# Half of the causal masks moved from a matmul to GpSimd, as a product on the exponentials' bits

## The reference

```
q = LN(x) @ Wq.T + bq ; k = ctx @ Wk.T + bk ; v = ctx @ Wv.T + bv
scores = einsum("bgrqd,bgkd->bgrqk", q, k) / sqrt(8)
scores = where(causal_mask, -inf, scores)      # 128 x 128, the same for all
scores = where(padding_mask, -inf, scores)     # 8 x 128, one row per batch
w   = softmax(scores)
x   = x + tanh(g_xattn) * ((w @ v) @ Wo.T + bo)
x   = x + tanh(g_ffn) * moe(LN(x))             # router, top 2 of 16, silu(gate) * up, down
```

## Time and profile before

| | us |
|---|---|
| median of three runs | 269.31 |
| span of the profiled execution (first to last instruction) | 267.6 |
| PE busy, share of the span | 237.8, 89% |
| DVE busy | 188.0, 70% |
| ACT busy | 96.7, 36% |
| POOL busy | 90.8, 34% |
| mean granted TensorE clock | 0.959 |

### The profile page before, as it was taken

How to read it: one execution, slowest core, us unless ns; L and a number is a source line. 1 busy time by engine, 2 the same in 40 slices (tenths; PEclk the granted TensorE clock), 3 DMA queues, 4 the chain that set the end, 5 groups by cost and what they waited for, 6 DMA issues and landing times.

```text
span 267.6 us, 3780 instructions
## 1 busy us (share of the span) xinstructions
PE 237.8 (89%) x1275; PEld 168.9 (63%) x1275; DVE 188.0 (70%) x388; ACT 96.7 (36%) x173; POOL 90.8 (34%) x103
## 2 busy tenths in 40 slices
PE   0874889897789999999968999989999999999993
PEld 0751345454546555556544588768888888888883
DVE  2689786958877777675793377769767665766565
ACT  1575023857746565564546521111111010101000
POOL 6266008030081417361160110406936633562000
PEclk9997556999999999999999999999999999999998
DMA  7945400001100000211011000001322102000004
GB/s 208 159 129 127 109 1 2 0 0 43 39 0 1 2 0 7 55 21 37 1 26 35 1 2 0 0 0 39 82 61 60 38 21 61 0 0 2 0 0 158
DMA packets 20595, 10.25 MB, mean 38 GB/s; under 512 B 14400, under 2 KB 20064, under 8 KB 20576
## 3 DMA queue, kind: packets, MB, share of 16 engines
q1 hardware_dynamic: 20272, 9.79, 15.5%
q10 hardware_dynamic: 304, 0.22, 0.3%
HBM read 7.91 MB, written 1.05 MB: 33 GB/s over the span
## 4 chain that ended last, share of the span: by engine, by line
PE 74%; DVE 14%; ACT 5%; issue 3%; DMA 2%; ACTq 0%; DVEq 0%
PE bank L878 66%; ACT q L527 3%; PE bank L939 2%; DMA wkv_n<-in_L_xattn_Wv 2%; DVE q L629 2%; PE bank L918 2%; DVE mneg L740 2%; PE bank L935 1%; DVE xn L620 1%; DVE x_sb L871 1%; DVE w L782 1%; PE bank L952 1%; DVE xT L626 1%; PE bank L944 1%; DVE k L629 1%
## 5 line engine op out<-in xcount | busy, mean ns | idle before, releaser
L878 PE MATMUL bank<-xT,cT 128*128 128x512 f32 x288 | 70.2, 392 | 0.0
L878 PEld LDWEIGHTS bank<-xT,cT 128*128 128x128 f32 x288 | 53.7, 188 | 12.0 <-issue 0.8
L740 DVE TENSOR_REDUCE mneg<-bank 128x4 f32<-128x512 f32 x64 | 43.7, 687 | 19.6 <-PE bank L878 18.9
L585 ACT ACTIVATE pT<-bank 128x512 f32<-128x512 f32 x64 | 38.3, 601 | 28.4 <-PE bank L878 27.3
L572 ACT ACTIVATE pT<-bank 128x512 f32<-128x512 f32 x24 | 14.4, 598 | 84.2 <-PE bank L878 84.2
L878 PEld LDWEIGHTS bank<-w_d,q 128*128 128x128 f32 x288 | 37.1, 188 | 2.8 <-issue 1.3
L878 PE MATMUL bank<-q,kz 112*128 112x512 f32 x64 | 38.8, 609 | 0.0
L878 PE MATMUL bank<-w_d,q 128*128 128x256 f32 x288 | 38.0, 281 | 0.8 <-DVE q L818 0.8
L878 PE MATMUL bank<-kz,q 96*128 96x512 f32 x64 | 30.6, 484 | 5.9 <-DVE mneg L740 3.2
L411 POOL TENSOR_TENSOR vare<-mv,cst 128x1 f32<-128x1 f32 (+1 forms) x10 | 1.9, 194 | 82.4 <-DVE mv L614 80.4
L878 PE MATMUL bank<-cmask,ident_b 128*128 128x512 bf16 x64 | 28.4, 444 | 0.0
(11 more groups left out here) (119 smaller groups left out, 312.0 us busy)
## 6 DMA issues: line engine op xcount, KB each, us to landing
padf<-in_L_ffn_down_w SPq DMA_DIRECT2D x12, 128.0 KB, 2.3
c_sb<-in_ctx SPq DMA_DIRECT2D x2, 512.0 KB, 7.3
q<-q SPq DMA_DIRECT2D x8, 128.0 KB, 2.4
out<-x_sb SPq DMA_DIRECT2D x4, 256.0 KB, 2.4
c_sb<-in_L_ffn_gate_w SPq DMA_DIRECT2D x8, 96.0 KB, 2.2
c_sb<-in_L_ffn_up_w SPq DMA_DIRECT2D x8, 96.0 KB, 2.2
x_sb<-in_x SPq DMA_DIRECT2D x2, 256.0 KB, 3.6
x_sb<-in_x SPq DMA_DIRECT2D x1, 512.0 KB, 8.0
```

The costliest lines, as they stand in the source:

```text
L585: nc.scalar.activation(pT[:, i // 4, i % 4, :], bank[2 + s % 2][:], ACT.Exp, scale=SCALE).then_inc(p_done, 1)
L740: nc.vector.tensor_reduce(mneg[:, r, 4 * hf:4 * hf + 4], bank[n % 2][:].rearrange("p (g k) -> p g k", g=4), X, ALU.max, negate=True).then_ ...
L878: return nc.tensor.matmul(dst, a, b, start=start, stop=stop, skip_group_check=True)
```

## The change

For groups 0, 2, 4 and 6 of each block (`BITS`), `scores_k` leaves its mask matmul out, and the matmul of the scores starts the bank. The exponential of a masked place is then some number and not 0. GpSimd multiplies the bits of `pT` of such a group, read as unsigned 32-bit integers, in place by `keep`, which holds 1 or 0 (`mask_bits`). `weigh_values` waits for these products too (`masked_ok`).

`keep` is made once: the padding mask is also loaded as 8 rows (`pad8_u`, a new DMA on SP), DVE turns it into floats, PE transposes it and the causal mask in a new job `mask` at slot 0, DVE compares both with -1 (0 or 1 out), and GpSimd multiplies them into 128 x 8 x 128 integers.

GpSimd's program is written in slots now: `separate_keys` in halves at slots 0 and 1 of a block, `mask_bits` in slots 0, 2, 4, 6, the split of gate and up at slots 3 and 5 of blocks 2, 4 and 6, of down at slot 3 of blocks 3, 5 and 7, the inverse deviation at slot 7, the clearing of `w_t` at slot 13, and the residual with its bias (`xb_sb`) one block at a time.

```diff
+BITS = (0, 2, 4, 6)
@@ SP
             sp.dma_start(mqk_u[:], m_qk).then_inc(d_mask, 16)
+            sp.dma_start(pad8_u[:], m_pad).then_inc(d_pad8, 16)
@@ GpSimd
+            def mask_bits(n):
+
+                pool.wait_ge(p_done, n + 1)
+                p = pT[:, n % G // 4, n % 4].bitcast(U32).rearrange("p (r q) -> p r q", r=R)
+                pool.tensor_tensor(p, p, keep[:, n // G].unsqueeze(1).to_broadcast([P, R, L]), ALU.mult).then_inc(masked_ok, 1)
...
+            pool.wait_ge(*emptied(("mask",)))
+            step(pool.tensor_tensor(keep[:], keep_q[:].unsqueeze(1).to_broadcast([P, NB, L]),
+                                    keep_p[:].unsqueeze(2).to_broadcast([P, NB, L]), ALU.mult))
...
-            pool.tensor_tensor(xb_sb[:], x_sb[:], bo_b[:].unsqueeze(1).to_broadcast([P, NB, D]), ALU.add).then_inc(xb_ok, 1)
+            for b in range(2):
+                pool.tensor_tensor(xb_sb[:, b], x_sb[:, b], bo_b[:], ALU.add).then_inc(xb_ok, 1)
...
-            for b in range(NB):
-                if b + KZ < NB:
-                    separate_keys(b + KZ)
...
+            for s in range(CH + G):
+                b, i = s // G, s % G
+                if i < 2 and b and b + KZ - 1 < NB:
+                    separate_keys(b + KZ - 1, i)
+                if s < CH and i in BITS:
+                    mask_bits(s)
+                if i == 4 and b + 2 < NB:
+                    pool.tensor_tensor(xb_sb[:, b + 2], x_sb[:, b + 2], bo_b[:], ALU.add).then_inc(xb_ok, 1)
...
+                if b in (2, 4, 6) and i == 3:
+                    split_hi(b // 2 - 1)
+                if b in (2, 4, 6) and i == 5:
+                    split_lo(b // 2 - 1)
+                if b in (3, 5, 7) and i == 3:
+                    split_down(b // 2 - 1)
+                if b and i == 7:
+                    inverse_deviation(NQ + b - 1, b - 1, 1)
+                if s in (ROUTE["best"][0] + 1, CH + G - 1):
...
                     pool.tensor_tensor(e2[:, t4], cst[:, C_E:C_E + TPH], dif[:, t4], ALU.pow).then_inc(e2_ok, 1)
@@ VectorE
+                elif k == "mask":
+                    nc.vector.tensor_scalar(keep_q[:], ps[:, 0:L], -1.0, None, ALU.is_ge)
+                    ins = nc.vector.tensor_scalar(keep_p[:], ps[:, L:L + NB], -1.0, None, ALU.is_ge)
...
+            ve.wait_ge(d_pad8, 16)
+            nc.vector.tensor_scalar(pad8[:], pad8_u[:], -BIG, None, ALU.mult).then_inc(pad_f, 1)
@@ TensorE
+                elif k == "mask":
+                    pe.wait_ge(masks_f, 1)
+                    pe.wait_ge(pad_f, 1)
+                    nc.tensor.transpose(ps[:, 0:L], mqk[:], ident)
+                    ins = nc.tensor.transpose(ps[:, L:L + NB], pad8[:], ident[0:NB, 0:NB])
...
-                mm(ps, cmask[:, b], ident_b[:].unsqueeze(1).to_broadcast([P, R, L]), True, False)
-                mm(ps, kz[0:KR, s, g], q4[0:KR, g // GH, :, toks(b)], False, True).then_inc(st_done, 1)
+                by_bits = n % G in BITS
+                if not by_bits:
+                    mm(ps, cmask[:, b], ident_b[:].unsqueeze(1).to_broadcast([P, R, L]), True, False)
+                mm(ps, kz[0:KR, s, g], q4[0:KR, g // GH, :, toks(b)], by_bits, True).then_inc(st_done, 1)
...
                 pe.wait_ge(p_done, G * b + 4 * hf + 4)
+                pe.wait_ge(masked_ok, masked_before(G * b + 4 * hf + 4))
```

More of the change, by code:

```diff
@@ L133, in build @@
         cmask = sb("cmask", [P, NB, L], BF16)
+        pad8_u = sb("pad8_u", [NB, L], U8)
+        pad8 = sb("pad8", [NB, L])
+        keep_q = sb("keep_q", [P, L], U32)
+        keep_p = sb("keep_p", [P, NB], U32)
+        keep = sb("keep", [P, NB, L], U32)
         bo_b = sb("bo_b", [P, D])
@@ L219, in build @@
         p_done = sem("p_done")
+        masked_ok = sem("masked_ok")
+        pad_f = sem("pad_f")
+        d_pad8 = sem("d_pad8")
         pv_done = sem("pv_done")
@@ L240, in build, with masked_before @@
                    ("q", 0, 0), ("q", 0, 1), ("c", 1, 0), ("c", 1, 1), ("MT", 0)]
-        AT_SLOT = {("vn", 0): 0, ("wo",): 8, ("x", 1, 0): 5, ("x", 1, 1): 6,
+        BIT_GROUPS = [n for n in range(CH) if n % G in BITS]
+        def masked_before(n):
+            return sum(m < n for m in BIT_GROUPS)
+        AT_SLOT = {("vn", 0): 0, ("mask",): 0, ("wo",): 8, ("x", 1, 0): 5, ("x", 1, 1): 6,
                    ("kv", 1): 3, ("q", 1, 0): 8, ("q", 1, 1): 11, ("vn", 1): 16}
@@ L443, in _ @@
                                mqk[:].unsqueeze(1).to_broadcast([P, NB, L]), ALU.add).then_inc(mask_ok, 1)
-            separate_keys(0)
-            separate_keys(1)
-            separate_keys(2)
+            for b in range(KZ):
+                for hf in range(2):
+                    separate_keys(b, hf)
             inverse_deviation(1, TPH, TPH)
+            pool.wait_ge(*emptied(("mask",)))
+            step(pool.tensor_tensor(keep[:], keep_q[:].unsqueeze(1).to_broadcast([P, NB, L]),
+                                    keep_p[:].unsqueeze(2).to_broadcast([P, NB, L]), ALU.mult))
             pool.wait_ge(tg_ok, 1)
@@ L492, in _ @@
             for t in range(WR, FT):
-                split_weights(t)
+                split_hi(t)
+                split_lo(t)
+                split_down(t)
         @block.scalar
@@ L687, in take @@
                     b = j[1]
-                    if b == 0:
-                        ve.wait_ge(xb_ok, 1)
+                    ve.wait_ge(xb_ok, b + 1)
                     ins = nc.vector.scalar_tensor_tensor(x_sb[:, b], ps[:, 0:D], tg[:, 0:1], xb_sb[:, b], ALU.mult, ALU.add)
```

45 lines of the change are left out of this document (23 added, 22 removed).

## The result

The changed kernel takes 273.79 us (median of four runs, 272.23 to 276.32); the kernel before, beside it on the same chip, 269.09 us (268.52 to 269.36). The ratio is 1.0151, 95% interval 1.0121 to 1.018, or some 4.1 us. The forecast was 267.3 us, faster; the time lies just above the range of 264.5 to 273.0 us.

What follows compares the result with a forecast made beforehand. PE was taken to bound blocks 2 to 5, DVE's chain the first half's router. Terms -5.17 - 0.6 + 1.2 + 0.8 + 1.3 + 0.3 + 0.2 = -1.97 us: span 265.6, median 267.3 us, range 264.5 to 273.

Steps and rivals of the forecast that it cites:

- The price of the product: One integer product on POOL: 1.27 us, with 1.04 as lower bound and 2.5 as upper.
- rival A: On POOL: the integer product is slow and POOL becomes the bound; 281 us at 2.2 us a product; chance 0.22.
- the last values of block 7: End of block 7: the last product against the last values, charged at +0.2 us.
- blocks 0 and 1: Block 0: DVE's waits beside POOL, +0.8 us (-0.3 to +3); block 1: two matmuls count, 0.47 us gained.
- the charge of 0.3 us per block for DVE's waits: Blocks 2 to 5: normalisation, cast and difference of `mt` wait for POOL, mostly hidden; +1.2 us in all.
- slot 19: PE's 0.98 us wait there mostly goes, as `w_t` is cleared at slot 13: -0.6 us (-0.98 to 0).
- the upper end: Blocks 2 to 5: the top of the range for DVE's waits on POOL, +3.2 us.
- rival B: DVE's waits on POOL in the blocks and router eat the gain; middle 271 us; chance 0.15.
- B's sign: In the profile after, PE would wait for `row_max` or `mt` behind stretched casts.
- The second term: Matmuls taken from PE: 0.235 us each, four per block all counting in blocks 2 to 5 (3.76 us); -5.17 us overall.
- The router: First half's router: a product ahead of `e2` delays DVE's chain, which PE awaits at CT: +1.3 us (+0.3 to +2.5).
- e2: POOL instruction at the router, 1.02 us, right behind `dif` before; forecast to stand behind one product of 1.27 us.

Runs made afterwards that it cites:

- xn_first: Changed kernel; from block 2 on GpSimd starts the product of slot 2 only after VectorE's normalisation of that block: 267.97 us, ratio 0.9923.
- slots_paced: Changed kernel without the product instructions, all 64 mask matmuls kept, GpSimd still waiting for each exponential at its place: 265.66 us, ratio 0.9856.
- no_products_paced: Changed kernel without the product instructions, 32 matmuls gone, those masks not applied, GpSimd still waiting for each exponential: 263.86 us, ratio 0.9791.
- bits_46: Changed kernel with products for groups 4 and 6 only, the other six masked by matmul: 265.56 us, ratio 0.9826.
- all_masks: Changed kernel with its products, but all 64 mask matmuls kept: 274.51 us, ratio 1.0164.
- bits_02: Changed kernel with products for groups 0 and 2 only, six masked by matmul: ratio 1.0057 (271.1 us) from three of nine runs; median of all 275.38.
- bits_0456: Changed kernel with products for groups 0, 4, 5 and 6 in place of 0, 2, 4 and 6: 269.35 us, ratio 0.9984.
- slots_only: Changed kernel without products and without their waits for exponentials, all 64 mask matmuls kept: 271.57 us, ratio 1.0096.
- no_products: Changed kernel without products and without their waits for exponentials, 32 matmuls gone, those masks not applied: 267.42 us, ratio 0.9927.
- gaps: Changed kernel with GpSimd waiting for its own completion after each product and each half of the keys: 269.17 us, ratio 0.9997.
- xn_first_gaps: Changed kernel with both edits, those of xn_first and of gaps: 269.10 us, ratio 0.9981.
- bits_456: Changed kernel with products for groups 4, 5 and 6 only, 24 of 64 mask matmuls gone: 267.52 us, ratio 0.9927.

## Why the prediction was wrong

**Held.** The price of the product (1.27 forecast, 1.286 us measured), and with it that rival A is out. That PE hardly waits for a product: the only wait is 0.21 us at the last values of block 7, charged at 0.2 (the view puts it down to the exponential; the last product ended at 152.42, 0.10 us before PE went on). That blocks 0 and 1 up to the `MT` of block 2 change by little (-0.4 us), though by luck: by the profiles above the new order gains there and the products lose about as much. That DVE's instructions from and to SBUF wait until POOL is done, but not only for the one instruction that is under way, as the prediction had it.

**The step that failed** is the charge of 0.3 us per block for DVE's waits, +1.2 us for blocks 2 to 5. It took three instructions as alike and leaned on `mt`, which has two slots of slack. The one that is hit is the normalisation, whose `YT` is next on PE. And the charge was made for a part of one POOL instruction; the normalisation stood at a place where POOL now has keys, product and split behind each other, and waited for two or three. A block from `YT` to `YT` takes 13.05, 13.45 and 13.02 us after, and 11.66 us in blocks 3 and 4 of xn_first, where that wait is gone: 1.5 us a block, five times the charge. At slot 19 the prediction even gave 0.6 us back, and the wait grew from 0.98 to 1.85 us. The doubt had been written down as the upper end (3.2 us for the blocks), and that was too low as well: four blocks at 1.5 us would be 6 us. It is rival B's mechanism, by B's middle (271 us) plus 2.8 us, though not by B's sign, which named `row_max` and `mt` and not the normalisation.

**The second term, too large:** the matmuls. 0.235 us each, all of them in blocks 2 to 5, made 0.94 us a block; the blocks show 0.50 and 0.44. The step "all count, as PE is full there" took a busy PE for one that waits for nothing. PE, block 4, before, is in the earlier trace rows; here is its end of slot 34 after the change, and ACT at the same time.

```profile
103.11 0.59 PE L928 MATMUL bank<-q,kz 112*128 112x512 f32 x1
...
104.47 0.39 PE L928 MATMUL bank<-cmask,ident_b 128*128 128x512 bf16 x1
104.96 0.63 PE L994 MATMUL bank<-cst,o_sb 128*128 128x128 f32 x4
```

```profile
103.74 0.60 ACT L631 ACTIVATE pT<-bank 128x512 f32<-128x512 f32 x1 [1.43 <-PE bank L928]
104.23 0.58 ACT L612 COPY o_sb<-bank 128x512 f32<-128x512 f32 x1
```

The job `TO` (L994) starts 0.15 us after ACT's copy of the previous block's output ended, and that copy stands behind the exponential of the scores at 103.11. Before, the same chain was as long: scores at 101.14, exponential 101.77, copy 102.26 to 102.84, `TO` at 102.98, while the matmul ahead of it came 0.25 us earlier at 102.73, so PE was full to the last moment. Between scores and `TO` stood the mask matmul that went (102.04), and what took its place is 0.25 us of waiting. The idle time is below what the view marks in brackets; one sees it only from the start times. The other half of the block loses some 0.17 us the same way at the other `TO` (100.41 to 100.81).

**The router** was charged +1.3 us. `e2` did come later, 2.84 us behind the `YT` of block 6 in place of 1.98, answering to the earlier trace rows:

```profile
136.66 1.28 POOL L461 TENSOR_TENSOR pT<-pT,keep 128x512 uint32<-128x512 uint32 x1 [0.71 <-ACT pT L631]
138.04 1.02 POOL L535 TENSOR_TENSOR e<-cst,dif 128x4 f32<-128x4 f32 x1
```

But from that `YT` to `CT` it took 7.79 us in place of 8.00, with two matmuls less. This net 0.3 us hides two terms: in slots_paced and no_products_paced the same stretch takes 6.93 and 6.94 us, so the new order gained 1.07 us there, which the prediction had not, and the products cost 0.85 us.

In sum: forecast -2.0 us, measured +3.5 us of span and +4.7 us in the medians. In the four steps from `MT` of block 2 to slot 43 the forecast had about -3.1 us (the -0.6, one matmul of block 1, and 0.94 less 0.3 for each of three and a half blocks); measured +4.5. All the rest was forecast at +1.1 and measured at -1.0.

**The whole, by single steps.** The two paced runs split the change into three, each a ratio to the kernel before: the order of POOL's program 0.9856 (-3.9 us), the 32 matmuls from there to 0.9791 (-1.8 us), the products from there to 1.0151 (+9.7 us). The forecast had next to nothing for the first (-0.6 at slot 19), -5.2 for the second and +3.8 for the products with DVE's waits and the start. So its three sizes were all wrong, and two of the errors nearly cancelled: what it missed in the order stands against what it saw too much in the matmuls. What the products cost decides the sign. xn_first takes 2.3% (6.1 us) of their 9.7 us away; what remains is at places other than the normalisation. By stretches of the profiles, in us:

| up to | before | slots_paced | no_products_paced | after |
|---|---|---|---|---|
| `MT` of block 1, from the start | 50.72 | 48.90 | 49.33 | 50.50 |
| `YT` in block 2, from there | 29.31 | 28.57 | 28.11 | 31.10 |
| `YT` in block 6, from there | 51.11 | 51.33 | 49.30 | 53.60 |
| `CT`, from there | 8.00 | 6.93 | 6.94 | 7.79 |

Between the last two columns 7.3 of 9.3 us of difference lie in the middle rows, where the normalisation is late and the clock fell.

**A version that beats both.** bits_46 (ratio 0.9826) and slots_paced (0.9856) can't be told apart by their intervals: with two products a block placed clear of the normalisation a kernel that applies all the masks takes 265.6 us. slots_paced has no product at all, so nearly all of the gain is that of POOL's order, not that of the matmuls. xn_first (0.9923) keeps all four products.

## What to carry over

In this kernel work handed to GpSimd was paid by VectorE where the two stood beside each other: look not at how full either is but at which VectorE instruction (both ends in SBUF) will be issued just ahead of or within the new work, and at who waits for that very instruction. Place the new work where VectorE reads PSUM, or let it wait for the critical VectorE instruction; here that one wait was worth over 2% (1.0151 to 0.9923). It did not make the products free: a run of the same program without them was another 1.3% faster. And when a change also reorders a program, time the new order alone first; here it was worth more than the work that was moved. A matmul taken from an engine that is busy for 99% of a stretch is worth its time only if no other chain is as long: compare start times at each cross-engine hand-over, not only the bracketed idle times.

## What was not expected of the hardware

How long VectorE is kept out depends on when it asks and on what GpSimd does next. Among the normalisations that met POOL with another instruction close behind, two groups stand out:

| issued | cases | let in | took |
|---|---|---|---|
| while a product is under way, 0.87 us or more before its end | all_masks blocks 3 to 6, bits_02 blocks 3 to 6, changed kernel block 6, bits_0456 block 7 | 0.15 us after that product's end, though another instruction follows at once | 1.02 to 1.32 us |
| while the keys are under way, 0.04 to 0.46 us before their end, and a product follows | changed kernel blocks 2 to 5, bits_02 block 2 | behind the product and the instruction after it | 2.00 to 2.84 us |

The second group as bits_02 shows it in block 2, DVE first: it waits for what is left of the keys, for the product and for L490.

```profile
83.46 2.84 DVE L666 TENSOR_SCALAR xn<-x_sb,mv,rstd 128x256 f32<-128x256 f32 x1
```

```profile
82.88 1.04 POOL L451 TENSOR_TENSOR kz<-k,cst 112x512 fp32r<-112x512 f32 x1
83.88 1.27 POOL L461 TENSOR_TENSOR pT<-pT,keep 128x512 uint32<-128x512 uint32 x1
85.11 1.04 POOL L490 TENSOR_TENSOR cT<-c_sb,zero 128x512 fp32r<-128x512 f32 x1
```

Four cases belong to neither group; they were passed over by one instruction: all_masks block 2 (issued 0.67 us before the keys' end, let in after the product, 2.05 us), xn_first block 2 (0.14 us before a product's end, keys next, 1.29 us), slots_only block 4 (0.04 us before, 1.41 us) and bits_0456 block 3 (0.10 us before, 0.82 us). Others issued 0.25 to 0.62 us before an end, with something else than a product next, were let in at that end: bits_0456 blocks 2 and 5, no_products blocks 2 and 4, slots_only block 2, and blocks 4 and 5 of the kernel before (0.70 us, at 103.77 and at 116.20).

The Trainium skill ("SBUF — State Buffer", section "Who interferes with whom") says that between GpSimd and a VectorE instruction in a 2-port mode whoever issues first holds the shared pair of ports for the whole instruction, and that the other blocks. For one instruction the runs agree (let in 0.15 us behind it). The second group goes beyond it: the normalisation was issued before the product and the one after it, and both went ahead.

What decides this between two instructions that follow each other closely is open; a gap that a semaphore makes let VectorE in wherever a normalisation stood waiting (gaps and xn_first_gaps, and L503 to L504 in the changed kernel's blocks 3 and 5). A clearing by GpSimd, which reads nothing, keeps VectorE out just as well (2.20 us for a cast of 0.18 us), and so does the integer product, whose price is that of a sum of reals of the same size (1.286 and 1.27 us).

The granted clock fell behind waits of PE: 0.57 in 70 to 74 us of the changed kernel behind 1.66 us of idling, though in the kernel before 1.41 us at the same place did not do it, nor 1.68 us in xn_first; in bits_0456 it fell to 0.59 behind 1.89 us, in bits_456 it stayed at 1.00 behind 1.87 us. What decides it is open. By the 9.45 and 8.07 us above, such a fall cost 1.4 us, in some of the profiles only.
